# Three stages on one core: a one-product projection and split value windows, a reordered VectorE slot, and an unrolled convolution chain with transfers issued one by one

## Time and profile before

| | |
|---|---|
| median of 3 runs | 25920.23 us (25901.7 to 25939.24) |
| profiled execution, its time | 25904.4 us |
| profiled execution, its span | 25902.2 us |
| TensorE busy | 25262.0 us, 98% |
| VectorE busy | 22974.0 us, 89% |
| ScalarE busy | 21932.0 us, 85% |
| GpSimd busy | 5686.5 us, 22% |
| mean granted TensorE clock | 0.994 |

### The profile page before, as it was taken

One profiled execution on the slowest core, in us unless ns is written; L12 is line 12 of the kernel. 1 busy time (PEld: TensorE's weight loads), 2 busy tenths in 40 slices (PEclk: granted clock), 3 DMA queues, 4 the chain that ended last, 5 costly groups with the idle time before them and its releaser, 6 DMA issues. The chain is left out here.

```text
span 25902.2 us, 756393 instructions
## 1 busy us (share of the span) xinstructions
PE 25262.0 (98%) x307482; PEld 14392.2 (56%) x307482; DVE 22974.0 (89%) x22334; ACT 21932.0 (85%) x18946; POOL 5686.5 (22%) x6562
## 2 busy tenths in 40 slices
PE   9999999999999999999999999999999999999899
PEld 5555555545545655654565455557545754555555
DVE  7777777799999999999999999999999999999222
ACT  7777777799999999999999999999999999998111
POOL 0000000033323322332333233223323332332000
PEclk9999999999999999999999999999999999999999
DMA  1111111388878888887888888888878888887665
GB/s 34 34 34 34 34 34 34 74 157 157 155 152 155 157 153 155 157 155 150 155 156 154 151 155 156 152 153 157 155 149 155 156 154 155 155 156 147 114 112 98
DMA packets 1515406, 3309.86 MB, mean 128 GB/s; under 512 B 543568, under 2 KB 675280, under 8 KB 1511632
## 3 DMA queue, kind: packets, MB, share of 16 engines
q0 software_dynamic: 770272, 2731.24, 58.3%
q1 hardware_dynamic: 742512, 536.70, 10.3%
HBM read 294.28 MB, written 201.33 MB: 19 GB/s over the span
## 5 line engine op out<-in xcount | busy, mean ns | idle before, releaser
L972 PE MATMUL surf_ps<-surf_u,surf_matf 64*64 64x512 f32 x87040 | 18777.3, 589 | 157.1 <-DVE surf_rest L1202 61.3
L977 PE MATMUL surf_ps<-surf_deriv,surf_matf 64*64 64x512 f32 x54400 | 11999.2, 590 | 0.1
L972 PEld LDWEIGHTS surf_ps<-surf_u,surf_matf 64*64 64x64 f32 x87040 | 7217.0, 133 | 7501.5 <-issue 6307.2
L977 PE MATMUL surf_ps<-surf_rest,surf_matf 64*64 64x512 f32 x32640 | 7232.4, 589 | 5.6 <-DVE surf_rest L1194 3.8
L1034 ACT ACTIVATE surf_deriv<-surf_ps 128x2048 f32<-128x2048 f32 (+1 forms) x2718 | 3927.4, 1445 | 655.0 <-PE surf_ps L977 648.9
L977 PEld LDWEIGHTS surf_ps<-surf_deriv,surf_matf 64*64 64x64 f32 x54400 | 3769.3, 133 | 656.5 <-issue 275.8
L1051 ACT ACTIVATE surf_rest<-surf_deriv 128x3072 f32<-128x3072 f32 x1360 | 3759.9, 2765 | 229.7 <-DVE surf_deriv L1155 220.0
L1097 POOL DMA_DIRECT2D surf_rest<-surf_rest x1360 | 1242.7, 914 | 8549.5 <-DVE surf_rest L1181 8168.7
L1181 DVE SCALAR_TENSOR_TENSOR surf_rest<-surf_rest,surf_deriv 128x2048 f32<-128x2048 f32 x1360 | 3106.5, 2284 | 0.3
L1194 DVE SCALAR_TENSOR_TENSOR surf_rest<-surf_deriv 128x2048 f32<-128x2048 f32 x1360 | 3106.4, 2284 | 0.0
L1108 POOL DMA_DIRECT2D surf_u<-surf_ds x2720 | 2294.4, 993 | 3590.0 <-DVE surf_ds L1208 3424.5
(11 more groups left out here) (111 smaller groups left out, 31142.6 us busy)
## 6 DMA issues: line engine op xcount, KB each, us to landing
surf_rest<-surf_rest POOLq DMA_DIRECT2D x3838, 512.0 KB, 5.8
surf_u<-surf_ds POOLq DMA_DIRECT2D x2720, 258.0 KB, 5.2
att_xin<-in_x SPq DMA_DIRECT2D x2048, 41.2 KB, 2.1
attended<-att_out_rows SPq DMA_DIRECT2D x1024, 64.0 KB, 2.0
surf_u<-attended SPq DMA_DIRECT2D x512, 128.0 KB
chain_us<-flowed SPq DMA_DIRECT2D x512, 128.0 KB, 3.8
chain_xs<-attended SPq DMA_DIRECT2D x512, 128.0 KB, 4.2
out<-chain_outs SPq DMA_DIRECT2D x504, 128.0 KB, 2.8
```

The source lines that it names most:

```text
L972: mm = pe.matmul(dst[out, bank(par, phase, CROSS, t), :], matf[rows, mat, :], u[rows, k, t, off + 2:off + 2 + W], start=(i == 0), stop=(i ...
L977: mm = pe.matmul(dst[out, bank(par, phase, DIAG, t), :], matf[rows, mat, :], field(*fields[i], rows=rows, lo=t * W + off, n=W), start=(i = ...
```

## The change

Attention: `project` is one product with the whole projection. Two new steps make its one input: ScalarE's `keep_even` copies the r = 0 half of `ps_o` times a 0/1 mask per partition into `even`, and VectorE's `keep_both` adds the r = 1 half times the other mask; `divide` is then one multiplication. `values` is issued in three parts, of 5, 2 and 1 windows. Surface: K is made before the clip of A and C and clipped after it; the clip of H goes to the end of the slot. Convolutions: TensorE's cycles are all written out (no loop) and so are SyncE's; TensorE increments `taps_passed` on the first matmul of each of the 24 tap groups of a cycle, and SyncE issues one load or store per group.

```diff
-                for w in range(half * WH, (half + 1) * WH):
+                for w in windows:
@@ project
-                for r in range(2):
-                    mm = pe.matmul(ps_m[0], w_proj[:, r, :], o_sb[:, par, r, :], start=(r == 0), stop=(r == 1))
-                mm.then_inc(proj_made, 1)
+                pe.matmul(ps_m[0], w_proj[:, :], o_sb[:, par, :], start=True, stop=True).then_inc(proj_made, 1)
@@ TensorE's slot
                 fc1(i - 3, o, 0)
-                values(i - 1, o, 0)
+                values(i - 1, o, range(0, 5))
                 fc1(i - 3, o, 1)
                 scores(i, par, 1)
+                values(i - 1, o, range(5, 7))
                 query(i + 1, (turn4 + 1) % 4)
                 key(i + 1, (turn4 + 1) % 4)
-                values(i - 1, o, 1)
+                values(i - 1, o, range(7, 8))
@@ ScalarE
+            def keep_even(i):
+                if not there(i):
+                    return
+                act.wait_ge(pv_made, i + 1)
+                wait(act, both_kept, i)
+                act.activation(even[:, :].rearrange("p (w n) -> p w n", n=N), ps_o[:, :, 0, :], ACT.Copy,
+                               scale=row_mask[:, 0:1]).then_inc(even_kept, 1)
...
                 split_v(i + 1, o)
+                keep_even(i - 1)
                 exps(i, par, 0)
@@ VectorE
+            def keep_both(i):
+                if not there(i):
+                    return
+                dve.wait_ge(even_kept, i + 1)
+                dve.wait_ge(pv_made, i + 1)
+                wait(dve, o_done, i)
+                dve.scalar_tensor_tensor(out=both[:, :].rearrange("p (w n) -> p w n", n=N), in0=ps_o[:, :, 1, :],
+                                         scalar=row_mask[:, 1:2], in1=even[:, :].rearrange("p (w n) -> p w n", n=N),
+                                         op0=ALU.mult, op1=ALU.add).then_inc(both_kept, 1)
@@ divide
-                for r in range(2):
-                    last = dve.tensor_tensor(o_sb[:, par, r, :].rearrange("p (w n) -> p w n", n=N), ps_o[:, :, r, :],
-                                             rec[:, :].rearrange("p (w n) -> p w n", n=N), ALU.mult)
-                last.then_inc(o_done, 1)
+                dve.tensor_tensor(o_sb[:, par, :], both[:, :], rec[:, :], ALU.mult).then_inc(o_done, 1)
@@ VectorE's slot
-                conv(i + 2, (turn4 + 2) % 4, range(0, 8))
+                conv(i + 2, (turn4 + 2) % 4, range(0, 6))
+                keep_both(i - 1)
+                conv(i + 2, (turn4 + 2) % 4, range(6, 8))
@@ surface, VectorE's slot
-                if here(s - 1) or here(s - 2):
-                    dve.wait_ge(copied_ac, s)
-                    clip_fields(*ac, by_dve(par), TW - by_dve(par)).then_inc(clipped_ac, 1)
                 if here(s - 4):
                     dve.wait_ge(rk_done, s - 3)
...
                                              op0=ALU.mult, op1=ALU.mult).then_inc(k_made, 1)
+                if here(s - 1) or here(s - 2):
+                    dve.wait_ge(copied_ac, s)
+                    clip_fields(*ac, by_dve(par), TW - by_dve(par)).then_inc(clipped_ac, 1)
+                if here(s - 4):
                     dve.wait_ge(k_made, s - 3)
                     clip_to(field("rK", par), 0).then_inc(k_clipped, 1)
@@ after h_made
-                    dve.wait_ge(h_made, s - 2)
-                    clip_to(field("rH", o), 1).then_inc(h_clipped, 1)
@@ after updated, the slot's last instruction
+                if here(s - 3):
+                    dve.wait_ge(h_made, s - 2)
+                    clip_to(field("rH", o), 1).then_inc(h_clipped, 1)
@@ convolutions
-        def every_cycle(eng, cycle):
+        def every_cycle(eng, cycle, unrolled=False):
...
-            for t in range(-1, 4):
+            for t in range(-1, LAST - 4 if unrolled else 4):
                 cycle(t, t % 4)
@@ SyncE
+            SHARE = 3 * 8
+            STORE_AT = range(7, SHARE, 2)
+            def cycle(t, r, passed):
+                total = groups_of(t)
+                loads, stores = 0, 0
+                for turn in range(SHARE):
+                    if turn < total:
+                        sp.wait_ge(taps_passed, passed + turn + 1)
+                        sp.sem_inc(paced, 1)
+                    if turn in STORE_AT and stores < 2 * B:
+                        store(t - 3, (r - 3) % 4, stores)
+                        stores += 1
+                    else:
+                        load(t + 4, r, loads)
+                        loads += 1
@@ TensorE, in across and along, first matmul of each group
+                                if not begun:
+                                    mm.then_inc(taps_passed, 1)
+                                    begun = True
```

More of the change, by code:

```diff
@@ L73, in attention_stage @@
         b_out = sb("b_out", [P, 1])
-        o_sb = sb("o", [P, 2, 2, T])
+        even = sb("even", [P, T])
+        both = sb("both", [P, T])
+        o_sb = sb("o", [P, 2, T])
         x2 = sb("x2", [P, 2, T])
@@ L249, in values @@
                                        start=True, stop=True)
-                if half:
+                if windows[-1] == WC - 1:
                     mm.then_inc(pv_made, 1)
@@ L582, in attention_weights @@
         [np.where(row == r, scale, 0).astype(f).reshape(128, 1) for r in range(2)] +
-        [np.where(head == h, 1, 0).astype(f).reshape(128, 1) for h in range(2)], axis=1).astype(f)
+        [np.where(head == h, 1, 0).astype(f).reshape(128, 1) for h in range(2)] +
+        [np.where(row == r, 1, 0).astype(f).reshape(128, 1) for r in range(2)], axis=1).astype(f)
     fc2 = blocks(np.ascontiguousarray(a["fc2_w"].T)).reshape(WR * HID // 128, 128, 128).transpose(1, 0, 2)
@@ L588, in attention_weights @@
         fc1=blocks(np.ascontiguousarray(a["fc1_w"].T)).reshape(128, 4, 128),
-        proj=np.stack([np.where((row == r)[:, None], blocks(np.ascontiguousarray(a["proj_w"].T)), 0).astype(f) for r in range(2)], axis=1),
+        proj=blocks(np.ascontiguousarray(a["proj_w"].T)),
         fc2=np.ascontiguousarray(fc2),
@@ L1276, in final @@
             return isinstance(m, int) and m == LAST
-        def every_cycle(eng, cycle):
-            for t in range(-1, 4):
+        def every_cycle(eng, cycle, unrolled=False):
+            for t in range(-1, LAST - 4 if unrolled else 4):
                 cycle(t, t % 4)
-            with eng.Fori(4, LAST - 7, 4) as t:
-                for k in range(4):
-                    cycle(t + k, k)
+            if not unrolled:
+                with eng.Fori(4, LAST - 7, 4) as t:
+                    for k in range(4):
+                        cycle(t + k, k)
             for t in range(LAST - 4, LAST + 3):
@@ L1317, in store @@
                 n, k = len(outs_of(m)), outs_of(m)[0]
-                for b in range(B):
-                    for s in range(2):
-                        rows = dst[b, :, bass.ds(m * (2 * G4) + (2 * k - 2 + s), 2 * n - 1), :]
-                        sp.dma_start(rows[:, 0:2 * n - 1:2, :],
-                                     outs[Q * b + C * s:Q * b + C * s + C, r % 2, k:k + n]).then_inc(stored[r % 2], 16)
-            def behind(made, m):
-                if there(m):
-                    sp.wait_ge(made, m + 1)
-                    sp.sem_inc(paced, 1)
@@ new lines, in store, with tap_groups, groups_of @@
+                sp.dma_start(rows[:, 0:2 * n - 1:2, :],
+                             outs[Q * b + C * s:Q * b + C * s + C, r % 2, k:k + n]).then_inc(stored[r % 2], 16)
+            def tap_groups(m, across):
+                if not there(m):
+                    return 0
+                return TAPS_X if across and final(m) else 2 * TAPS_X
+            def groups_of(t):
+                return tap_groups(t, False) + tap_groups(t - 2, True) + tap_groups(t - 2, False) + tap_groups(t + 1, True)
+            SHARE = 3 * 8
@@ L1342, in _ @@
             for t in range(3):
-                for quarter in range(4):
-                    load(t, t, quarter)
+                for part in range(4 * B):
+                    load(t, t, part)
                 if t == 0:
                     sp.wait_ge(loaded[0], 2 * LOADS)
-            every_cycle(sp, cycle)
-            store(LAST, LAST % 4)
+            passed = 0
+            for t in range(-1, LAST + 3):
+                passed = cycle(t, t % 4, passed)
+            for part in range(2 * B):
+                store(LAST, LAST % 4, part)
@@ L1426, in cycle @@
                 conv4(t - 2, (r - 2) % 4, 1)
[L1428 removed]
+            every_cycle(pe, cycle, unrolled=True)
         @block.scalar
```

69 lines of the change are left out of this document (35 added, 34 removed).

## The result

The changed kernel takes 25477.67 us (median of 4 runs, 25471.74 to 25491.19) against 25915.56 us for the kernel before (4 runs, 25901.7 to 25939.24): ratio 0.9834, interval 0.9822 to 0.9846. So 438 us are gone where 545 were forecast. The time lies inside the range, 103 us above the forecast.

The account below looks back on a forecast made before the run. TensorE's instruction list was taken to bound attention and most surface slots, VectorE the near slots; convolutions lost time to jumps and loads. Savings of 325 + 55 + 165 = 545 us gave about 25375 us, range 25260 to 25600.

Parts of the forecast that it names:

- The mechanism of attention: Attention: TensorE's list sets the slot; less work and moved windows shorten it by 1.32 us, from 19.11 to near 17.8.
- the product: Attention: one projection product less saves 0.955 us per slot, less a new wait of about 0.1 us.
- the moves: Attention: windows of `values` moved into TensorE's waits for the gelus win 0.75 us per slot, of which 0.47 stays.
- rival 5: Attention: the slot does not shorten, since ScalarE with the copy takes over; 25700 us, chance 0.05.
- The failed step: Attention: 1.27 us per slot over 256 chunks, some loss in filling and draining slots included, gives -325 us.
- the term: Surface: the new order frees 0.24 us of VectorE in each of 242 near slots, -58 us, taken as -55.
- rival 2: Attention and surface: only removed work counts, moved windows return as waits, VectorE finds another wait; 25598 us, chance 0.15.
- Jumps: Convolutions: 13 loop jumps of 5.9 us each go away with TensorE's loop, -77 us.
- Spreading: Convolutions: issuing transfers one by one instead of in clusters saves 1.5 us in each of 58 cycles, -88 us.
- rival 1: Convolutions: spreading does nothing, because loads cost by their traffic and not their clusters; 25463 us, chance 0.18.
- 4: Convolutions: spread transfers disturb TensorE's instruction supply at many places, making the kernel slower; 26190 us, chance 0.03 with like mishaps.
- The counting of groups: Convolutions: semaphore updates on 24 matmuls per cycle, priced at nothing, with 42 us as the other end.

Follow-up runs that it names:

- 1: Changed kernel with 36 one-instruction semaphore increments of TensorE ahead of its attention loop: 25454.56 us, ratio 0.9827.
- 2: Kernel before with 220 one-instruction semaphore increments of TensorE ahead of its attention loop: 25987.52 us, ratio 1.0031.
- 3: Changed kernel with 116 one-instruction semaphore increments of TensorE ahead of its attention loop: 25397.05 us (1 run).
- 6: Changed kernel with VectorE's surface slot in the old order, K and H clipped right behind their making: 25465.28 us, ratio 0.9835.
- 10: Changed kernel with TensorE's attention and surface loops written out: 25332.61 us, again 25344.47; the same with the old surface order 25344.22.
- experiment 4: Changed kernel with SyncE's convolution transfers issued in clusters as before, TensorE's cycles still written out: 25608.85 us (1 run).
- experiment 5: Changed kernel with TensorE's convolution cycles in a loop of 4 as before, transfers still spread: 25477.91 us (1 run).

## Why the prediction was right and wrong

**The mechanism of attention held.** The ordinary slot was forecast at about 17.8 us and is 17.87, 1.21 shorter. The parts were less exact than their sum: the product 0.91 (0.86), the moves 0.32 (0.47); added they make 1.23, measured together 1.21, where the step had 1.32. ScalarE's idle time before the exponential is 0.11 us (0.2 forecast), so rival 5 was closer than it looked, and still false. `divide` with `keep_both` fits as forecast: the residual still waits, and 1.02 us where 0.5 was expected.

**The failed step is what is missing from it:** "For 256 chunks, with some loss in the filling and draining slots: 1.27 x 256". I priced the jump of TensorE's loop in the convolutions, where it goes away, and did not ask about the one in attention, where it stays, since it cost 0.6 us there. 229 = 325 - 77 (84 - 7 at the jumps) - 19 for the slots being 1.21 instead of 1.27 shorter and the ends. The experiments show that its price depends on where the loop's ends lie (1, 2, 3), in either kernel, and to 0.73 us on how much work is queued ahead of the jump (3). The Trainium skill ("Runtime: NRT & Kernel Launch", section "Instruction fetch mechanics") says that instructions come in blocks of 16 KB, ahead and in sequence, and that a taken branch to a block that is not there waits for its fetch. The trace's packets of 16384 bytes agree, and so does the packet inside every branch. That a second standstill follows, since the target lies near the end of its block and the next one was not yet on the way, no page states; the packet that lands inside the second standstill at each of the 11 jumps shows it, and experiments 1 to 3 move it away and bring it about.

**Surface: the term fails.** The step priced the edit at 242 x 0.24 and leaned on the 58.1 us that TensorE waited for H. That wait did go (16.5), and nothing came of it. The near slots lie at the change of group, where the units are loaded too. If TensorE is through sooner, it waits for the units instead, and the near slots keep their mean though their median fell by 0.26 us; rival 2 named this ("VectorE finds another wait") in the wrong place. Experiments 6 and 10 show the exchange, 63.9 + 20.9 against 16.5 + 86.5 and 65.3 + 53.9 against 22.5 + 80.4 us; the sums vary from execution to execution as the units' wait does. What sets the units' time, how much of it is the transfers and how much the wait for their buffers, was not tried.

**Convolutions: right direction, the size low.** Jumps 77 by the forecast, 70 by experiment 4. Spreading: "I take half and a little more, 1.5 us in 58 cycles: -88"; it is 2.4 us in each, 142. Without jumps a cycle takes 27.7 us with clusters (experiment 4), 25.3 with spread transfers and 24.56 without loads: three quarters of the loss was the clusters. What holds the last 0.7 us, the traffic or the straight code (the loop's ordinary cycles in experiment 5 take 24.9), stays open. Rivals 1 and 4 fall by this: with one transfer for each tap group TensorE stood for issue 15 times in 1540 us. The counting of groups, taken at nothing, does cost nothing: 24.62 and 24.50 us in the last cycles without loads against 24.46 and 24.56 before. The Trainium skill's sentence (same section) that fetching straight code is hidden behind the pace of issue does not hold here with clustered transfers (77 us of standing in experiment 4, all in straight code) and agrees for spread ones (6.5 us).

**Range and chances.** Against the forecast the convolutions gave 47 us more, attention 96 less and the surface stage 64 less, 113 in sum. So the time lies in the range partly by luck: two terms that were too large were offset by one that was too small. Luck even more is the time of rival 1, 25463, only 15 us from the measured one. Its claim, that spreading does nothing, is refuted by 142 us; its sum comes out near only because it leaves out a gain that happened and keeps two that did not happen in full. Rival 2 (25598) lies 120 us off, and its reason was right in the surface stage alone.

## What to carry to other kernels

When work is taken out of a hardware loop, look at the slot that holds the jump back apart from the others, before and after: its price can change by a factor of ten from a shift of its place alone (0.6 to 6.6 us in experiment 2). Unrolling took it away here, and padding with no-ops most of it. Do not count a wait as a gain before asking what the engine meets next in that same stretch; the sum of its waits over the stage is what has to fall. Issue DMA transfers one by one between pieces of work rather than in clusters, since here a cluster also delayed the supply of instructions (77 us of standing against 6.5).

## What the runs showed of the hardware

- A jump back of TensorE costs 0.6 us (before), 1.7 (116 increments), 3.9 (36) or 7.6 us (after) in the same loop, by its place. In the last of these part is standing, 41.8 us at 11 jumps, and the rest fits the clock: 0.50 is recorded for about 10 us at the jump near 1646 us, of which 8.3 are work done at half speed, so some 4 us lost. The clock stayed at 1.00 after 0.79 us of standing; in the changed kernel it fell at 1647.0 us, behind a standstill of 1.45 us and 0.2 us into the next. With one standstill of 2.1 to 2.7 us (36 increments) it fell at seven jumps of eleven, after one of 2.15 us but not after one of 2.47: the length alone does not decide.
- The branch takes 3.4 to 3.9 us in attention, in either kernel, with one 16384-byte packet of instructions landing inside it; 4.3 to 4.8 us when a second packet is under way at the same time.
- In the convolutions of the kernel before the jump did the same. PE's timeline and the window around it:

```profile
24464.26 5.52 PE L1381 MATMUL chain_ps<-chain_hidden,chain_w 32*32 32x512 f32 x96 [3.96 <-issue]
```

```profile
24460.00:24485.00 25.00, 21.04 (x585) 14.29 (x581) 8.25 (x5) 1.97 (x1) 0.00 (x0) 0.86 0.40 85
```

  The 5.9 us that the forecast read off a jump cycle were thus 3.96 of standing and, I conclude, 2 of a halved clock (the window's mean of 0.86 is 0.14 x 25 = 3.5 us of full clock lost, a part of which fell into the standing).
- Transfers of 128 KB issued in clusters make TensorE stand with nothing to wait for in straight code, 117 times in the stage and up to 2.5 us (experiment 4); the same transfers one per microsecond hardly do (15 times). 116 of the 117 end 1.2 to 1.9 us after a packet of instructions has landed.
- Single executions of one kernel differ by 24 us in a stage (surface: 18854.5 and 18878.3 us for one kernel), and eight kernels with the same code in the surface stage by 29 us (18895.5 to 18924.2). So an effect of 50 us is read in its stage and not in one total, and one of 20 us in neither without repeats.
